# Vision tower with routed experts on one core: later weight split, new order around the heads, one block for both phases

## What is computed

```python
h  = concat([cls_tok, class_token, patches @ W_lin.T + b_lin]) + positions   # 64 x 38 x 256
# mLSTM block, on xn = layernorm(h)
x_mlstm, z = split(xn @ W_up)
x_act = swish(causal_conv4(x_mlstm)); q, k, v = headwise(x_act, x_act, x_mlstm)
ig, fg = [q, k, v] @ W_ig + b_ig, [q, k, v] @ W_fg + b_fg
Dmat = exp(logD - max(logD)); C = q k^T / sqrt(128) * Dmat
hn = headnorm((C / norm) v)
h  = h + ((hn * norm_w + skip * x_act) * swish(z)) @ W_down
# feed-forward, on xn2 = layernorm(h): one shared expert, one routed expert (top 1 of 32)
base = h + (silu(xn2 @ sg) * (xn2 @ su)) @ sd
out  = base + expert[e](sigmoid(top) * xn2)          # e = argmax(xn2 @ gate_w)
```

## Time and profile before

| | |
|---|---|
| median of 3 runs | 744.8 us |
| lowest, highest | 743.41, 746.59 us |
| profiled execution, its own time | 744.39 us |
| its span, first to last instruction | 742.6 us |
| PE busy | 657.5 us (89%) |
| DVE busy | 469.3 us (63%) |
| ACT busy | 390.6 us (53%) |
| POOL busy | 227.6 us (31%) |
| granted TensorE clock, mean, of full speed | 0.931 |

### The profile page before, as it was taken

The page is one execution under the profiler, slowest core; times in us unless marked ns, Lnnn a source line. Parts: engine busy times, 40 slices in busy tenths (PEclk is TensorE's granted clock), DMA queues, the critical chain, the costliest instruction groups (busy, mean ns, idle before and its releaser), DMA issues. The chain is left out here.

```text
span 742.6 us, 11751 instructions
## 1 busy us (share of the span) xinstructions
PE 657.5 (89%) x4013; PEld 556.0 (75%) x4013; DVE 469.3 (63%) x1529; ACT 390.6 (53%) x856; POOL 227.6 (31%) x249
## 2 busy tenths in 40 slices
PE   4868999899999999899899978858599999999992
PEld 3757878878878878878878857737388888888782
DVE  1543666766766766766766763654567676767660
ACT  1335729629629629629629528302366666666660
POOL 3000011133033033133133133243356664312541
PEclk9698689999999999999999997977799999999997
DMA  8149010020020020020010010042599999999860
GB/s 307 64 124 359 24 49 1 18 83 18 18 82 19 18 82 19 18 81 19 19 33 20 18 32 16 18 137 102 174 369 379 378 380 375 322 409 345 292 241 15
DMA packets 46261, 101.69 MB, mean 137 GB/s; under 512 B 10952, under 2 KB 32246, under 8 KB 41329
## 3 DMA queue, kind: packets, MB, share of 16 engines
q1 hardware_dynamic: 35184, 89.07, 33.1%
q0 software_dynamic: 9488, 8.52, 4.4%
q10 hardware_dynamic: 1520, 3.23, 1.3%
HBM read 80.17 MB, written 23.32 MB: 139 GB/s over the span
## 5 line engine op out<-in xcount | busy, mean ns | idle before, releaser
L407 POOL TENSOR_TENSOR rstd_h<-var_h,minus_half 76x4 f32<-76x4 f32 x32 | 32.3, 1010 | 223.2 <-DVE var_h L844 223.2
L1671 POOL DMA_INDIRECT out<-rows,bg x32 | 37.5, 1171 | 72.0 <-DVE rows L1741 65.2
L1843 PE MATMUL bank<-w_hi,x_hi 128*128 128x512 f32 x148 | 57.6, 471 | 1.9 <-DVE x_lo L1753 1.9
L1075 PE MATMUL bank<-patch,lin_w 128*128 128x288 f32 x192 | 51.9, 424 | 7.8 <-DMA col_t<-cols 7.8
L451 ACT ACTIVATE att_t<-bank 128x304 f32<-128x304 f32 x16 | 6.8, 423 | 88.0 <-PE bank L1226 87.3
L1075 PEld LDWEIGHTS bank<-patch,lin_w 128*128 128x128 f32 x192 | 37.6, 200 | 18.2 <-POOL v L384 7.8
L748 DVE SCALAR_TENSOR_TENSOR y<-xm,conv_t,y 128x296 f32<-128x296 f32 (+2 forms) x96 | 44.3, 512 | 10.7 <-ACT xm L451 10.7
L1843 PE MATMUL bank<-w_lo,x_hi 128*128 128x512 f32 x148 | 47.0, 399 | 0.0
L1843 PE MATMUL bank<-w_hi,x_lo 128*128 128x512 f32 x148 | 46.6, 396 | 0.0
L1747 DVE TENSOR_TENSOR w_lo<-wts,w_hi 128x1024 fp32r<-128x1024 f32 x36 | 43.1, 1217 | 0.2 <-ACT w_hi L1794 0.2
L1466 POOL DMA_INDIRECT x_zone_dram<-xs_rows,spot x32 | 37.6, 1175 | 16.1 <-issue 8.9
(11 more groups left out here) (251 smaller groups left out, 1790.9 us busy)
## 6 DMA issues: line engine op xcount, KB each, us to landing
wts<-w_exp SPq DMA_DIRECT2D x18, 1024.0 KB
x_act<-w_exp SPq DMA_DIRECT2D x10, 1024.0 KB
silu_z<-w_exp SPq DMA_DIRECT2D x9, 1024.0 KB
wts_down<-w_exp SPq DMA_DIRECT2D x18, 512.0 KB
patch<-patches SPq DMA_DIRECT2D x8, 864.0 KB, 6.5
down_w<-w_exp SPq DMA_DIRECT2D x10, 512.0 KB
lin_w<-w_exp SPq DMA_DIRECT2D x9, 512.0 KB
b_zone_dram<-act_t SPq DMA_DIRECT2D x1, 4160.0 KB, 28.5
```

What stands on the lines that cost most here:

```text
L407: pool.tensor_tensor(rstd_h[:, j, :], var_h[:, j, :], minus_half[:], ALU.pow).then_inc(s_rstdh, 1)
L1075: last = pe.matmul(fb[c][:, 0:GS * N], lin_w[:, k, c * 128:(c + 1) * 128], patch[:, k, :], start=(k == 0), stop=(k == KF - 1))
L1671: pool.indirect_dma_start(out, bass.IndirectOffsetOnAxis(ap=rows_at, axis=0), rows[:, k % 4, :], None, bounds_check=T - 1, oob_is_err=Fals ...
L1843: last = pe.matmul(banks[2 + 2 * e + u][:, :], x[:, e, c * SLOT:(c + 1) * SLOT], w[:, e, u, c * I:(c + 1) * I], start=(n == 0), stop=(n == ...
```

## The change

1. *Shared weights.* The raw shared weights get a tile of their own, `sgu_raw`; the raw head weights go to `y` and `att_t`. `split_shared` moves on ACT and DVE from the end of step 1 to the end of step 2. The copy into q_t moves into `merge_weights`, `centre_values` moves ahead of DVE's `embed`, and turning the up weights uses banks 6 and 7. Each wait of the first group's stage a names the part of the preparation that it needs.
2. *Order around the heads.* PE: heads 2 and 3 and up 5 come before gate_up 1; the mixed gates and up 6 before ranks; the first of the four `q_of` products of the next group before att_rows. DVE: all four `weigh` before expert_act 0.
3. *One block.* Both phases share one `nc.Block()`, with no barrier between them. The last group's stage m on ACT and DVE becomes a list of its own (`last_group`), called from slot 0, with three halves of expert weights split in between. SP's last stores and first loads are interleaved (`last_rows`). `late_rows` runs after slot 1's activation; filling the table (`table_of`) stays ahead of slot 0. The slots use other PSUM banks, and the tiles that are dead in the last step are placed first, so that the slots' tiles take their room.

The bodies of both phases also move one level to the left. The diff without that, cut to its core:

```diff
@@ groups_phase, tiles
+        sgu_raw = sb("sgu_raw", [128, KD, 2 * I])
-        sgu_raw = [buffer.rearrange("p k n -> p (k n)")[:, 0:2 * I] for buffer in (hst[:], q_t[:].rearrange("p h j t -> p h (j t)"))]
-        q_raw = within(raw_qk, "p k n -> p (k n)", 0, [KI, 128])
+        q_raw = within(y, "p k s t -> p (k s t)", 0, [KI, 128])
...
@@ groups_phase, SP
+            def last_rows(which):
+                if which == 0:
+                    sp.wait_ge(s_h2, 2 * G)
+                    sort.first_loads(sp, w_exp)
+                elif which == 1:
+                    sp.wait_ge(s_xs, NT * G)
+                    dst = dram.xs[(G - 1) * GT:, :].rearrange("(j p) d -> p j d", p=R)
+                    sp.dma_start(dst, xs_rows[:]).then_inc(s_xs_out, 16)
+                else:
+                    sp.wait_ge(s_base, 2 * G)
+                    dst = dram.base[(G - 1) * GT:, :].rearrange("(j p) d -> p j d", p=R)
+                    sp.dma_start(dst, base_rows[:, :, 0:D]).then_inc(s_base_out, 16)
@@ groups_phase, ACT
                 def step(e, f, a, m):
+                if final(e, f, a):
+                    return
...
-                    if f and f.n == 0: split_shared()
+                if f and f.n == 1: split_shared()
+            def last_group(split):
+                m = Group(G - 1, (G - 1) % 2)
+                split(0, 0)
+                xn2_t_of(m)
+                split(0, 1)
+                tanh_score(m)
+                silu_g_of(m, 0)
+                silu_g_of(m, 1)
+                score_rows(m)
+                silu_g_of(m, 2)
+                split(1, 0)
+                silu_g_of(m, 3)
+                ffn_t_of(m)
@@ groups_phase, DVE
+                dve.wait_ge(s_prep, 11)
+                dve.tensor_copy(q_t[:, :, :, R:], gx_w[:].unsqueeze(2).broadcast_to([128, NH, NT, 2 * NH])
+                                ).then_inc(s_prep, 1)
...
                         weigh(a, 0)
                         weigh(a, 1)
+                    weigh(a, 2)
+                    weigh(a, 3)
                     if m:
                         expert_act(m, 0)
                         score_of(m)
-                    if a:
-                        weigh(a, 2)
-                        weigh(a, 3)
...
+                if f and f.n == 0: centre_values()
                     if e: embed(e)
...
-                        centre_values()
-                        split_shared()
-                        put_gate_columns()
+                if f and f.n == 1: split_shared()
+            def last_group(split):
+                m = Group(G - 1, (G - 1) % 2)
+                ln2_stats(m)
+                xn2_of(m)
+                split(0, 0)
+                xn2_lo_of(m)
+                route(m)
+                choose(m)
+                expert_act(m, 0)
+                score_of(m)
+                expert_act(m, 1)
+                rank_of(m)
+                split(0, 1)
+                expert_act(m, 2)
+                split(1, 0)
+                expert_act(m, 3)
+                dve.wait_ge(s_past, G)
+                sort.count_slots(dve)
+                base_of(m)
+                sort.table_of(dve)
@@ groups_phase, PE
-                        pe.wait_ge(s_prep, PREP_ALL)
-                    for h in range(NH):
+                    pe.wait_ge(s_prep, 12)
+                for h in heads_at:
                         if h < 2:
-                            wait(pe, s_att, KD * a.n)
+                        wait(pe, s_att, KD * (a.n - 1) + h + 1)
                         else:
                             wait(pe, s_h2, 2 * a.n)
...
-                    if a: q_of(a)
+                if a: q_of(a, range(1, NH))
...
                         heads(a, 0)
                         heads(a, 1)
+                if f: up(f, 5)
+                if a:
+                    heads(a, 2)
+                    heads(a, 3)
+                if m: gate_up(m, 1)
+                if f:
+                    if f.n > 0: mixed_gates(f)
+                    up(f, 6)
                     if m:
-                        gate_up(m, 1)
                         ranks(m)
                         gate_up(m, 2)
...
-                    if a:
-                        heads(a, 2)
-                        heads(a, 3)
-                    if f: up(f, 5)
                     if m: gate_up(m, 3)
-                    if f:
-                        if f.n > 0: mixed_gates(f)
-                        up(f, 6)
-                        up(f, 7)
+                if f: up(f, 7)
                     if m: shared_down(m)
...
-                    if a:
-                        down(a)
-                        att_rows(a)
+                if a: down(a)
+                if f: q_of(f, range(0, 1))
+                if a: att_rows(a)
@@ experts_phase, SP
+            sort.last_rows(0)
+            load_gate_up(2, sort.load, 2)
+            sort.last_rows(1)
                 sp.wait_ge(sort.s_x_put, 16 * TILES)
                 load_x(0)
                 load_x(1)
-                for k in (2, 3):
-                    load_gate_up(k, sort.load, k)
+            load_gate_up(3, sort.load, 3)
                 load_x(2)
                 load_x(3)
+            sort.last_rows(2)
                 sp.wait_ge(sort.s_b_put, 16 * TILES)
@@ experts_phase, DVE, turn(k); ACT alike with sort.last_act(w_hi_of)
                     if k == 0:
-                        w_lo_of(0, 0)
+                    sort.last_dve(w_lo_of)
                     x_lo_of(k)
                     if k > 1:
                         rows_of(k - 2)
+                if k > 0:
                     w_lo_of(k, 1)
-                    if k + 1 < E:
+                if k == 0:
+                    pass
+                elif k + 1 < E:
                         w_lo_of(k + 1, 0)
...
+                if k == 1:
+                    sort.late_rows(dve)
```

More of the change, by code:

```diff
@@ L58, in sem @@
             return ctx.enter_context(nc.semaphore(name))
+        up_hi = sb("up_hi", [128, KD, 2 * INNER], f32r)
+        up_lo = sb("up_lo", [128, KD, 2 * INNER], f32r)
+        sgu_raw = sb("sgu_raw", [128, KD, 2 * I])
+        patch = sb("patch", [128, KF, GS * N])
+        h_t = sb("h_t", [128, KD, GS, S])
+        xm = sb("xm", [128, 2, KI, GS, S])
+        y = sb("y", [128, KI, GS, S])
+        xn = sb("xn", [R, NT, D])
+        xn_hi = sb("xn_hi", [128, KD, GT], f32r)
+        xn_lo = sb("xn_lo", [128, KD, GT], f32r)
+        q_t = sb("q_t", [128, NH, NT, QW])
+        c_t = sb("c_t", [R, NT, NH, QW])
+        v = sb("v", [R, NT, INNER])
+        h_rows = sb("h_rows", [R, 2, NT, D])
+        pick = sb("pick", [AT, NT * NH, R], f32r)
         ident = sort.ident
@@ L1238, in route @@
                     if m.n == 0:
                         pe.wait_ge(s_prep, 24)
-                    for j in range(NT):
-                        tile = slice(j * R, (j + 1) * R)
-                        for c in range(KD):
-                            pe.matmul(mb[0][0:R, 2 * j * E:2 * (j + 1) * E], xn2_hi[:, c, tile], route_w[:, c],
-                                      start=(c == 0), stop=False)
-                        for c in range(KD):
-                            last = pe.matmul(mb[0][0:R, 2 * j * E:(2 * j + 1) * E], xn2_lo[:, c, tile],
-                                             route_w[:, c, 0:E], start=False, stop=(c == KD - 1))
@@ L1281, in shared_down @@
-                def shared_down(m):
-                    pe.wait_ge(s_act, KI * m.n + KI)
-                    for c in range(KD):
-                        for k in range(KI):
-                            last = pe.matmul(mb[c][:, 0:GT], sd_w[:, k, c * 128:(c + 1) * 128], act_t[:, k, :],
-                                             start=(k == 0), stop=(k == KI - 1))
-                        last.then_inc(s_sd_mm, 1)
-                def ffn_rows(m):
-                    pe.wait_ge(s_ffn, KD * m.n + KD)
-                    to_rows(mb, ffn_t, s_ft_mm)
@@ L1357, in _, with shared_down @@
-                pipeline(pe, step)
+                else:
+                    pe.wait_ge(s_sg, KI * m.n + k)
+                for u in range(2):
+                    if u and k:
+                        pe.wait_ge(s_act, KI * m.n + k)
+                    if u and k == 2:
+                        pe.wait_ge(s_own, m.n + 1)
+                    at = u * I + k * 128
+                    split_product(mb[u][:, 0:GT], (sgu_hi, sgu_lo), (xn2_hi, xn2_lo), at).then_inc(s_gu_mm, 1)
+            def shared_down(m):
+                pe.wait_ge(s_act, KI * m.n + KI)
+                for c in range(KD):
+                    for k in range(KI):
+                        last = pe.matmul(mb[c][:, 0:GT], sd_w[:, k, c * 128:(c + 1) * 128], act_t[:, k, :],
+                                         start=(k == 0), stop=(k == KI - 1))
+                    last.then_inc(s_sd_mm, 1)
@@ L1360 @@
+            pipeline(pe, step)
 class Sort:
@@ L1514, in late_rows, with table_of @@
```

(1 more changed line is left out.)

2186 lines of the change are left out of this document (1089 added, 1097 removed).

## The result

The change made the kernel 1.5% slower: 755.6 us (median of 4 runs, 752.93 to 758.25) against 744.2 for the kernel before on the same chip; ratio 1.0148, 95% interval 1.010 to 1.0195. I had forecast 739.3, and 728 to 747. The profiled execution took 757.17 us, its span is 755.5, 12.9 more than before.

The account below looks back on a forecast made before the run. TensorE is busy 89% of the span, but the change can move only PE's idle time outside the slots. Terms -8.4 + 1.0 + 0 + 1.2 - 1.9 + 2.6 = -5.5 us gave 739.3 us, range 728 to 747.

Parts of the forecast that it names:

- Start-up: Before PE's first head product: 5.52 us gap goes, products and transposes behind it run faster; -8.4 us, lower end -5.5.
- the two terms for the clock: At start-up, low clock behind the gap goes: 2.0 us on four head products, 0.9 on eight transposes.
- Split shared weights: Subtractions moved a step later on DVE, behind h2 and ahead of the statistics: +1.0 us, ends 0 and +2.6.
- Steady steps: Six steps with all stages: three short PE waits become one of some 2.4 us before shared_down; 0, ends -3 and +4.
- the term for spells of low clock: In half of the six steady steps, a low-clock spell no longer covered by a wait costs some 1.2 us.
- rival 3: Slower: the 2.4 us wait drops TensorE's clock each steady step, about 4 us each time; 763 us, chance 0.09.
- My point from which it decides: In steady steps, the low-clock rival decides from 1.5 us a step: 9 us over the sum, over 748.5 us.
- Step without a new group: Step with heads but no up product: two heads before gate_up 1 shift DVE's chain; +1.2 us, ends 0 and +1.7.
- Hand-over: Groups to experts: xn_lo 2.7 us late, yet first gathered rows load earlier; -1.9 us, ends -4.6 and -0.4.
- Late rows: Behind slot 1's expert_act, 3.1 us on DVE delay x_lo and slot 2, 0.5 slack; +2.6 us, ends +2.2 and +3.1.
- Rival 1: PE bounds the steady steps: three waits go without a new one, 1.8 us six times; 728 us, chance 0.10.
- Rival 2: Saving eaten by later weight landings, late rows, moved subtractions and low start-up clock; 742 to 746 us, chance 0.16.

## Why the prediction was wrong

- **Start-up, -8.4.** Measured -5.25. The 5.52 us of the gap went, the two terms for the clock (2.0 and 0.9) did not come: I had laid the low clock to the gap, and it falls there without that gap too. My lower end, -5.5, was about right.
- **Split shared weights, +1.0.** Measured 0, my lower end. xn itself was only 4.0 us ahead, at 112.31, but ACT's two table loads in front of xn_hi had come the full 5.3 earlier, and xn_lo follows those.
- **Steady steps, 0, ends -3 and +4.** Measured about +14 (0.3 up to the first shared_down and 13.8 for five intervals). This is the step that failed: the term for spells of low clock. The wait itself was sized nearly rightly (2.4, measured 2.64). The step without a spell was put at 55.4 and took 55.9, because expert_act 3 came 1.95 us later behind the shared_down before it and not 1.4; that is 1.1 us of the 13.8. The other 12.7 are spells, in two parts. I gave half of the steps one spell of low clock at a cost of 1.2, which by my own working came to +2.4 in all, and then took 0 without a reason; measured were 27.2 us at the lower level in five steps, each us costing almost a half. And I counted only spells that were there before, while the wait makes its own: this is the mechanism of rival 3, to which I had given 0.09. Filling the wait took away 6.6 us, about half of the loss; the other half are spells in the decays, longer than before and no longer covered by a wait. Rival 3's price was smaller than I had put it: 3.4 us at the lower level and 1.7 us lost behind four of six waits, not 4 us of loss behind each. My point from which it decides, 1.5 us a step more than forecast, is passed with 2.8. The reason I gave against it, that steps with several short waits held 1.00, was no evidence on one long wait.
- **Which chain.** "Expert_act 1 on DVE waits for gate_up 1, and from it DVE runs without a pause" was true as a row and wrong as a cause. In the changed kernel two paths meet in one place: the ranks' calculation on DVE ended at 255.35, and gate_up 2 on PE at about 255.4 by the profile, whose matmul ends are modelled. It took three runs to find the second.
- **Step without a new group, +1.2.** Measured +3.9. The part that I had in mind, DVE's chain shifted behind two heads, is in the wait ahead of shared_down (1.88 for 0.63); the rest came near the start of the step, where heads_t waited 2.02 us for DVE instead of 0.54, and the clock was low for 6.8 us behind that instead of 3.4.
- **Hand-over, -1.9.** From the end of h2 to slot 0's gate_up 31.9 us instead of 35.3: -3.4. The weights were asked for at 508.85 and taken up at 513.87, 5.0 us, between my 6.0 and the estimate of 4.4. The Trainium skill, DMA: Bandwidth & Descriptors, section Anatomy of one DMA, gives the figures behind that estimate for a DMA issued from GpSimd, and SP issues this one; I had not said so. So xn_lo came 1.7 us late and not 2.7. Slot 0 then ran at full clock, where the earlier trace rows stood in a spell, for another 1.8.
- **Late rows, +2.6.** Measured 2.6 from slot 1 to slot 2, and 1.7 for the spell behind the wait, which I had not counted.
- **Rival 1** fell: steps under 55 us came only with another order of PE than the change has. **Rival 2** fell too: of its costs only the low clock at start-up came (2.9 us), while the weights landed earlier than I had put them and the late rows cost my middle value.

The Trainium skill, TensorE: Matmul & The Clock Gate, section HAM oscillation, describes waits between bursts of products after which the next burst starts at half rate. The trace agrees in kind, with shorter waits than the page describes: of six equal waits of 2.64 us four were followed by 1.2 GHz. The page does not say which ones.

## What to carry to other kernels

Before filling a short wait of the bounding engine, ask what the filler stands ahead of: here three waits of 0.6 to 1.0 us were exchanged for one of 2.6, by putting the heads ahead of a product (gate_up 2) from which another engine's long chain starts. Where a row shows an engine without a pause, look for every release that falls within it, not only the one at its head; cutting one of two equal paths gains nothing. And here time at the lower clock was nearly free only in steps that held a wait for it to use up, so a reordering that removes such waits should be judged by a step with a spell in it.

## What the runs showed of the hardware

- Equal waits had unequal effects: at six waits of 2.64 us the clock fell four times in the changed kernel and six times with gate_up 1 early, at six of 2.5 us three times, behind waits of 1.06 and 1.30 us in the steady steps never.
- The clock also fell where PE waited for nothing, during the short products of the decays (at 238.4 us in the changed kernel, with no wait of PE over 0.1 us in the 6.9 us before), and the length varied between equal steps (0, 3.4 or 6.8 us). Kernels with a wait of 1.30 us had such a spell in nearly every step, the two with steps of 54.6 and 54.7 us in none. What sets it off stays open; no run separated it.
- At start-up the products of the changed kernel ran at the lower clock from 50.7 to 57.5 us although PE was busy all that time; the last wait before it took 0.78 us.
